# A transformer block with attention and a mixture of experts: a new prelude that builds the first stack on the chip and leaves the rest to the loop

## What is computed

```python
xn = layernorm(x)                                # x is (8, 512, 128): 8 batches of 512 tokens
q, k, v = xn @ Wq.T, xn @ Wk.T, xn @ Wv.T         # 16 heads of 8
q, k = rope(q), rope(k)                          # the angle depends on the batch alone
att = softmax(q @ k.T / sqrt(8)) @ v             # per batch and head
s = sigmoid(xn @ gate_w.T)                       # 32 experts in 8 groups
combine = top 6 experts of the best 4 groups of s + e_bias, weights s / sum * 2.5
moe = sum_e combine_e * relu(xn @ up_e.T)**2 @ down_e.T
shared = relu(xn @ shared_up.T)**2 @ shared_down.T
out = x + att + moe + shared
```

## Time and profile before

| | us |
|---|---|
| median of 3 runs | 686.49 (686.17 to 690.81) |
| the profiled execution | 682.6 |
| its span, first to last instruction | 680.8 |
| TensorE busy in it | 664.0 |
| DVE, ACT, POOL busy | 426.9, 414.4, 421.5 |

### The profile page before, as it was taken

How to read it: one execution, slowest core, us unless ns; L and a number is a source line. 1 busy time by engine, 2 the same in 40 slices (tenths; PEclk the granted TensorE clock), 3 DMA queues, 4 the chain that set the end, 5 groups by cost and what they waited for, 6 DMA issues and landing times. The chain is left out here.

```text
span 680.8 us, 12599 instructions
## 1 busy us (share of the span) xinstructions
PE 664.0 (98%) x4450; PEld 311.2 (46%) x4450; DVE 426.9 (63%) x1055; ACT 414.4 (61%) x771; POOL 421.5 (62%) x461
## 2 busy tenths in 40 slices
PE   7988999999999999999999999999999999999996
PEld 6532444445444444444444444445444444454443
DVE  5783567566865777566765777667756686655300
ACT  2534356665666666666666666766666566666662
POOL 1570347765787567665776668666676576656654
PEclk9997599999999999999999999999999999999999
DMA  7826034543246335633446314734555314332320
GB/s 197 272 78 187 23 72 94 192 124 95 59 110 215 77 76 125 222 95 94 113 108 195 83 44 120 222 94 94 125 159 157 94 43 110 88 79 62 94 64 16
DMA packets 52974, 77.80 MB, mean 114 GB/s; under 512 B 6064, under 2 KB 19248, under 8 KB 52784
## 3 DMA queue, kind: packets, MB, share of 16 engines
q1 hardware_dynamic: 52336, 75.95, 41.7%
q10 hardware_dynamic: 576, 1.05, 0.5%
HBM read 57.19 MB, written 19.40 MB: 112 GB/s over the span
## 5 line engine op out<-in xcount | busy, mean ns | idle before, releaser
L648 DVE TENSOR_REDUCE nmax<-sc 128x1 f32<-128x512 f32 x512 | 330.4, 686 | 195.3 <-PE sc L806 190.7
L472 ACT ACTIVATE probs<-st 128x512 f32<-128x512 f32 x512 | 278.0, 595 | 49.7 <-PE st L822 48.4
L364 POOL TENSOR_TENSOR gated<-gate_at,relu 128x512 f32<-128x512 f32 x128 | 163.3, 1276 | 206.7 <-ACT relu L477 206.7
L368 POOL TENSOR_TENSOR g<-gated,relu 128x512 f32<-128x512 f32 x128 | 163.0, 1274 | 18.5 <-POOL gated L364 0.4
L477 ACT ACTIVATE relu<-upb 128x512 f32<-128x512 f32 x128 | 76.5, 597 | 139.5 <-PE upb L877 139.5
L822 PE MATMUL st<-stacks 32*128 32x512 f32 x512 | 152.8, 575 | 0.0
L847 PE MATMUL acc<-dn,g 128*128 128x128 f32 x1024 | 149.2, 289 | 1.4 <-POOL g L368 1.4
L847 PEld LDWEIGHTS acc<-dn,g 128*128 128x128 f32 x1024 | 124.7, 192 | 45.6 <-issue 44.0
L806 PE MATMUL sc<-stacks 32*128 32x512 f32 x512 | 140.2, 501 | 1.0 <-DVE nmax L648 1.0
L841 PE MATMUL pv<-probs,v_aug 128*32 128x512 f32 x1024 | 138.1, 612 | 0.0
L877 PE MATMUL upb<-xnT,up 128*128 128x512 f32 x256 | 134.0, 606 | 0.0
(11 more groups left out here) (102 smaller groups left out, 399.0 us busy)
## 6 DMA issues: line engine op xcount, KB each, us to landing
gate_at<-gate_rows SPq DMA_DIRECT2D x64, 512.0 KB, 6.5
q_stack<-qk_parts SPq DMA_DIRECT2D x32, 256.0 KB, 6.4
stacks<-q_stack SPq DMA_DIRECT2D x32, 256.0 KB, 4.6
stacks<-k_stack SPq DMA_DIRECT2D x32, 256.0 KB, 5.1
k_stack<-qk_parts SPq DMA_DIRECT2D x28, 256.0 KB, 5.6
gate_at<-in_x SPq DMA_DIRECT2D x8, 256.0 KB, 5.2
x_res<-in_x SPq DMA_DIRECT2D x8, 256.0 KB, 7.0
out<-y SPq DMA_DIRECT2D x8, 256.0 KB, 6.9
```

Of the source, the lines that this page charges most:

```text
L364: nc.gpsimd.tensor_tensor(gated[:, u % 2, :], gate_at[:, group % RING, u % GATES, :], relu[:, u % RELUS, :], ALU.mult).then_inc(gated_read ...
L368: nc.gpsimd.tensor_tensor(g[:, u % 2, :], gated[:, u % 2, :], relu[:, u % RELUS, :], ALU.mult).then_inc(g_ready, 1)
L472: nc.scalar.activation(probs[:, u % 2, h, :], st_b[h % 2][:], ACT.Exp).then_inc(probs_ready, 1)
L648: nc.vector.tensor_reduce(out=nmax[:, s % 2, at:at + 1], in_=sc_b[tile % SC_BANKS][:], op=ALU.max, axis=AXX, negate=True).then_inc(s_read, 1)
```

## The change

The first stack (batch 0, heads 0 to 3) is no longer sent through DRAM. POOL copies the weight columns of its heads four times (`replicate`), PE projects batch 0 with these into rows that already stand in the stack's order (`project_rows`), and DVE writes high or low part of each row by two passes (`first_stack`). The other three stacks of batch 0 still go through DRAM.

Only batches 0 and 1 are transposed and projected in the prelude. Batches 2 to 7 follow in the loop, two batches ahead: transposes in unit 0, q in 4, k in 8, logits in 15; the shared products stand in 7 and 11, v in 3, gates in 12. x of batches 3 to 7 is loaded in the loop; its statistics are taken in units 10 and 11 on DVE, and the inverse root and normalisation in 11 to 14 on POOL, with an exponent of -0.5 (`inverse_std`). The router's gates of batch 0 are computed from piece 4 on in units 0 to 2 and turned in unit 3. The down products start in unit 6 and catch up by two in every second unit (`place_downs`); `RELUS` is 8. Four scores of step 1 are ahead of the loop and not eight, and the first four units take six each.

The sigmoid is now an exponential, an addition of one (`logits_out`), and a reciprocal on DVE in piece 0 of the route. Three operations of the route use a form that also writes an accumulator (`apart`).

```diff
-RELUS = 4
+RELUS = 8
...
-LAG = 2
+LAG, FIRST_LAG = 2, 6
...
-FIRST_AHEAD = 8
+FIRST_AHEAD = 4
+
+FIRST_X = 3
...
+def place_downs():
+
+    done = 0
+    for u in range(FIRST_LAG, UNITS):
+        due = u - LAG + 1
+        n = 2 if u >= FIRST_LAG + 2 and u % 2 == 0 else 1
+        while done < due and n:
+            DOWN_AT[u].append(done)
+            done += 1
+            n -= 1
+
...
+        SHDOWN_UNIT = (4, 6)
+        SQUARE_UNIT, SPLIT_UNIT = (7, 15), (5, 6, 9, 10)
...
+        X_UNIT, V_UNIT, Q_UNIT, K_UNIT, SH_UNIT, GATE_UNIT, LOGIT_UNIT = 0, 3, 4, 8, (7, 11), 12, 15
+
+        V1_UNIT, GATE0_UNIT = 1, 3
...
+        STATS_UNIT, AGGR_UNIT, LN_UNIT, NORM_UNIT = 10, 11, 11, (12, 13, 14, 14)
+
+        ROUTE_MID, ROUTE_END = {3: 2, 4: 3, 7: 5, 8: 6}, {0: 0, 2: 1, 6: 4, 8: 7, 10: 8}
+        ROUTE1_MID, ROUTE1_END = {6: 2, 7: 3, 8: 5, 10: 6}, {4: 0, 5: 1, 7: 4, 10: 7, 11: 8}
+
+        ROUTE0_FIRST, ROUTE0_MID, ROUTE0_END = 4, {1: 5, 2: 7}, {0: 4, 1: 6, 2: 8}
+        ROUTE_AT = (0, 3, 6, 8, 9, 12, 14, 15, 19, 21)
         ROUTE_PIECES, ROUTE_STEPS = len(ROUTE_AT) - 1, ROUTE_AT[-1]
 
 
...
+        WARM_FIRST, WARM_COPY, WARM_CHAIN = 30, 6, 10
+
+        BESIDE = (("v", 0), ("shared", 0), ("shared", 1), ("x", 1), ("q", 1), ("k", 1), ("logits", 1))
+        NW1, NW2, NUP, NALL = 4, 3, 5, 7
...
+            store_rows(0, 0, slice(QUAD, 2 * QUAD), stored_1)
+            store_rows(0, 1, slice(QUAD, 2 * QUAD), stored_1)
+            store_rows(0, 0, slice(2 * QUAD, H), stored_2)
             load_stack(0, 1)
-            sp.dma_start(up[:], upT).then_inc(w2_ld, 16)
+            store_rows(0, 1, slice(2 * QUAD, H), stored_2)
+            load_max(0)
+            load_stack(0, 2)
+            load_stack(0, 3)
             sp.dma_start(sdn[:], shared_down.rearrange("(n p) d -> p n d", p=P)).then_inc(w2_ld, 16)
             sp.dma_start(dn[:], down.rearrange("(n p) d -> p n d", p=P)).then_inc(w2_ld, 16)
-            load_stack(0, 2)
-            load_stack(0, 3)
+            store_parts(1)
+            load_x(FIRST_X)
...
+                    if s == 0:
+                        store_gates(0)
+                        load_gates(0)
...
+            def replicate(w):
+
+                nc.gpsimd.tensor_copy(w_rows[:, w, :].rearrange("p (h c d) -> p h c d", c=COPIES, d=HD),
+                                      (wq, wk)[w][:, 0:QUAD * HD].rearrange("p (h d) -> p h d", d=HD).unsqueeze(2)
+                                      .to_broadcast([P, QUAD, COPIES, HD])).then_inc(rows_ready, 1)
+
+            def inverse_std(batches, first):
+
+                at = slice(batches[0] * TT, (batches[-1] + 1) * TT)
+                n = at.stop - at.start
+                v, inv, p0, t0 = (ln[:, k, at] for k in range(4))
+                step = [first]
+
+                def then(ins):
+                    step[0] += 1
+                    ins.then_inc(ln_step, 1)
+                    pool.wait_ge(ln_step, step[0])
+
+                pool.wait_ge(var_ready, batches[-1] + 1)
+                then(nc.gpsimd.tensor_scalar(v, mv[:, at, 1], 1.0, EPS_LN, ALU.mult, ALU.add))
+                then(nc.gpsimd.tensor_tensor(p0, v, half[:, 0:n], ALU.pow))
+                then(nc.gpsimd.tensor_tensor(t0, p0, p0, ALU.mult))
+                then(nc.gpsimd.tensor_tensor(inv, t0, v, ALU.mult))
+                then(nc.gpsimd.tensor_scalar(t0, inv, -0.5, 1.5, ALU.mult, ALU.add))
+                then(nc.gpsimd.tensor_tensor(inv, p0, t0, ALU.mult))
+
+            def normalise(i, tiles):
+                if i < FIRST_X:
...
+            pool.wait_ge(xn_first, 1)
+            set_v(0)
+            pool.wait_ge(half_ready, 1)
+            inverse_std((1, 2), 0)
+            for k in range(4):
+                split(0, k)
+            normalise(1, range(TT))
+            for i in range(NSH):
+                square(0, i)
+            normalise(2, range(TT))
+            set_v(1)
             for k in range(4):
                 split(1, k)
...
+                if b + FIRST_X < B:
+                    if n == LN_UNIT:
+                        inverse_std((b + FIRST_X,), (b + 1) * LN_STEPS)
+                    tiles = [k for k in range(TT) if NORM_UNIT[k] == n]
+                    if tiles:
+                        normalise(b + FIRST_X, tiles)
...
+            def logits_out(i):
+
+                act.wait_ge(logit_psum, i + 1)
+                tiles = sig[:, i * TT:(i + 1) * TT, :].rearrange("p t e -> p (t e)")
+                nc.scalar.activation(tiles, up_b[:, 0:TT * NE], ACT.Exp, scale=-1.0).then_inc(exp_ready, 1)
+                act.wait_ge(exp_ready, i + 1)
+                nc.scalar.activation(tiles, tiles, ACT.Copy, bias=1.0).then_inc(sig_ready, 1)
...
+            def first_stack(w):
+
+                dve.wait_ge(rows_psum, w + 1)
+                dve.wait_ge(low_ready, 1)
+                src, rows = (pv_b, acc_b)[w], stacks[:, 0, w, :]
+                nc.vector.tensor_scalar(rows, src[:], low_fac[:, w:w + 1], None, ALU.mult).then_inc(stack_low, 1)
+                dve.wait_ge(stack_low, w + 1)
+                nc.vector.scalar_tensor_tensor(rows, src[:], fac[:, w:w + 1], rows.bitcast(F32), ALU.mult, ALU.subtract
+                                               ).then_inc(stack_set, 1)
+
+            def apart(out_at, src, scalar, op):
+
+                return nc.vector.tensor_scalar(out_at, src, scalar, 0.0, op, ALU.max, accum_out=junk[:])
...
+                    then(nc.vector.reciprocal(sig[:, tiles, :], sig[:, tiles, :]))
...
-                    then(nc.vector.tensor_scalar_add(msk[:, :, 0:NE], tmp[:], 0.0))
+                    then(apart(msk[:, :, 0:NE], tmp[:], 0.0, ALU.add))
...
+            for i in (1, 2):
+                stats_of(i)
+                moments(i).then_inc(var_ready, 1)
...
+            cut_max(dve, nc.vector, 0)
...
+            def project_rows(w):
+
+                pe.wait_ge(rows_ready, w + 1)
+                nc.tensor.matmul((pv_b, acc_b)[w][:], w_rows[:, w, :], xnT[:, 0:T], start=True, stop=True
+                                 ).then_inc(rows_psum, 1)
...
+            warm(WARM_FIRST, sc_b[0])
+            transpose_x(0)
+            warm(WARM_COPY, sc_b[0])
+            pe.wait_ge(w_ld, NW1 * 16)
+            pe.wait_ge(xnT_ready, 1)
+            project_rows(0)
+            project_rows(1)
+            project(0, 0)
+            project(0, 1)
+            logits(0)
+            for i in range(TILES // 2):
+                score(2 * i)
+                score(2 * i + 1)
+                for kind, k in BESIDE[i:i + 1]:
+                    beside(kind, k)
+            pe.wait_ge(exp_ready, 2)
             max_transpose(0)
+            pe.wait_ge(qk32_ready, 4)
+            warm(WARM_CHAIN, acc_b)
             for i in range(FIRST_AHEAD):
                 score(TILES + i)
-                for kind, n in BEHIND[i * len(BEHIND) // FIRST_AHEAD:(i + 1) * len(BEHIND) // FIRST_AHEAD]:
-                    prelude(kind, n)
-            pe.wait_ge(qk32_ready, 2 * (B - 1))
...
+            warm(WARM_CHAIN, acc_b)
+            pe.wait_ge(m_ready, 1)
...
+                if u == V1_UNIT:
+                    make_v(1)
+                if u == GATE0_UNIT:
+                    gate_transpose(0)
...
+                if b + 2 < B:
+                    if n == X_UNIT:
+                        transpose_x(b + 2)
+                    if n == Q_UNIT:
+                        project(b + 2, 0)
+                    if n == K_UNIT:
+                        project(b + 2, 1)
+                    if n == LOGIT_UNIT:
+                        logits(b + 2)
+                couple(u, 1)
+                if u == 0:
+                    pe.wait_ge(w2_ld, NUP * 16)
+                if u == FIRST_LAG:
+                    pe.wait_ge(w2_ld, NALL * 16)
+                for e in DOWN_AT[u]:
+                    expert_down(e)
+                if u == FIRST_LAG:
+                    for i in range(NSH):
+                        shared_down(0, i)
+                if b and n in SHDOWN_UNIT:
                     shared_down(b, SHDOWN_UNIT.index(n))
```

More of the change, by code:

```diff
@@ L46 @@
 MAXES = MAX_PARTS
-LAG = 2
+LAG, FIRST_LAG = 2, 6
 SC_BANKS = 3
 AHEAD = 12
-FIRST_AHEAD = 8
+FIRST_AHEAD = 4
+FIRST_X = 3
+LN_STEPS = 6
 SC_HEAD = (2, 3, 0, 1)
 SC_AT = {}
+DOWN_AT = {u: [] for u in range(UNITS)}
 def place_scores():
@@ L64, in place_scores @@
         if u < TT:
-            left = min(left, QUAD + 1)
-        for h in range(QUAD):
-            n = -(-left // (QUAD - h))
-            SC_AT[u, h] = list(range(at, at + n))
+            left = min(left, QUAD + 2)
+        for couple in range(2):
+            n = -(-left // (2 - couple))
+            SC_AT[u, couple] = list(range(at, at + n))
             at += n
@@ L543, in then, with stats_of, moments, invert_first @@
                 dve.wait_ge(link, done[0])
[L545 to L559 removed]
+            def stats_of(i):
+                dve.wait_ge(x_ld[i], 16)
+                at = i * TT if i < FIRST_X else 0
```

(62 more changed lines are left out.)

457 lines of the change are left out of this document (194 added, 263 removed).

## The result

| | before | after |
|---|---|---|
| median of 20 runs, us | 687.26 (686.08 to 690.81) | 692.01 (687.28 to 696.46) |
| the profiled execution | 682.6 | 687.3 |
| its span | 680.8 | 685.2 |
| granted clock over the span, profiled run | 0.977 | 0.975 |

A forecast was written before the change was run, and what follows sets the result against it. TensorE's own work was taken to bound mid-loop, half clock and the first stack's DRAM trip the start. 67.0 + 579.8 + 17.9 = 664.7, clock +8 gives span 672.7, offset to the median: forecast 676.5, range 666 to 690.

The forecast's parts named there:

- the wait behind step 0: After step 0's sixteen scores, PE waits 2.7 us for the transpose of the maxima, longer than the 1.89 before.
- the clock's fall there: PE's clock halves at the wait near 29.8, returns in unit 1, may fall again in units 2 and 3: +8 us.
- The insertions: Work for batches 3 to 7 put into loop units, 0.24 of each hidden: 2.6 us a batch, 12.9 in all.
- the sum: Full-clock time of the changed kernel: 67.0 to unit 5's product, 579.8 behind it, 17.9 added: 664.7 us.
- the 579.8 us of before: Old span from unit 5's product at 101.0 to the end at 680.8, tail included, reused for the changed kernel.
- just enough: GpSimd catching up to lag 2 by unit 14: 13 products of 2.6 and 9 us other work in 45 us.
- The second term: the reciprocal: Reciprocal over 128 columns on DVE in route piece 0: 0.25 in each of seven batches, +1.7, bounds 0 and 4.5.
- The accumulating form: In route piece 4, keeps DVE off the port shared with GpSimd, removing a 0.65 stall in six batches: -3.9 us.
- rival 4: GpSimd's power between gating 11 and 12 in five batches costs 5.8 us or more each: 693.5 us; chance 0.10.
- half of an offset: The median shown lay 3.9 us above the profiled run; +2 was carried into the forecast.
- Rival 1: PE stays at half speed from the start until the down products in unit 6: 683.5 to 689.5 us; chance 0.28.
- Rival 3: In the loop, insertions are not hidden and DVE still stalls: 9.7 us above forecast, 686; chance 0.10.

The follow-up runs named there:

- experiment 3: Changed kernel without the reciprocal over 128 columns in the first route piece (routing differs); one profiled run, 680.15 us.
- Experiment 2: Changed kernel with the cuts of the maxima of steps 2 and 3 on GpSimd, not DVE; 682.66 us, ratio to before 0.9942.
- experiment 11: Changed kernel with GpSimd's products of experts 1 and 6 held back until DVE has written cuts 2 and 3; one profiled run, 690.94 us.
- experiment 4: Changed kernel with the three route operations in plain form again, without accumulator; one profiled run, 693.98 us.
- experiment 5: Changed kernel with the power on GpSimd done four times, not once, in each inverse root; one profiled run, 715.4 us.
- experiment 1: Changed kernel with 22 warm-up transposes filling TensorE's wait behind step 0's scores; 690.29 us, ratio to before 1.0048.
- experiments 2 and 9: The latter: changed kernel, cuts on GpSimd, early exponential table, 22 warm-ups in the gap, eight in each of units 0 to 3, route pieces respread; 675.63 us, ratio 0.9825.

## Why the prediction was wrong

**Right.** The first projection (10.7; 11.20) and first score (15.3; 15.62), the wait for the exponential (0.9; 1.22), the wait behind step 0 (2.7; 2.30), the clock's fall there and its price: unit 5's product at 75, measured 74.2. Up to there 27 us are gained, 26 were reckoned. The insertions: x 0.35 (0.36 forecast), q and k 0.82 each (0.82). One power hidden. The stall of 0.65 in unit 5 is gone, and `msk` near 0.25 (0.29). In part the 74.2 is luck. Unit 3's product came at 64.46, where the sum has 59.3 and 8 for the clock, and units 4 and 5 then took 9.7 us for the 7.7 of the sum, 0.86 of it by the reciprocal that stands before unit 5 (experiment 3). Nor was DVE without idle in units 0 to 3: from 57.3 to 64.1 it was busy for 4.72 of 6.80. (Two slips of the sum, 59.8 carried on as 59.3 and a product at 72.3 called 5.5 and not 5.3 later, change nothing.)

**The step that failed first: the stretch behind unit 5's product.** I took the 579.8 us of before and added work to it, as if batch 0 from unit 6 on were in the state it had at 101.00. It is not. Before, GpSimd's first products waited for the relus, one pair a unit (line 364 at 70.62, 77.28 and 87.57), and the cuts of these steps were GpSimd's own, in order with them. The change gives those of batch 0 to DVE. The gates, forecast for 67.6, came 5.6 us later, and the products start at 73.2, one behind the other, just as DVE has to cut the maxima of step 2. I wrote that GpSimd was "just enough" and never asked what DVE does beside it. The cut stood in the sum as 1.55 to 1.7; it takes 3.3. With the row maxima behind it, that makes two waits of 1.78 and 1.70 and 3.4 us at the half clock, which cost 1.7: 5.5 us in unit 6 (the three terms give 5.2), and 2.0 in unit 10, behind a wait of 1.88. Experiment 2 gets 5.8 of these back (7.56 and 5.54), experiment 11 shows the cause, and experiment 3 shows unit 6 without the meeting (8.01). The Trainium skill says it outright, SBUF — State Buffer, Who interferes with whom: a DVE instruction with two inputs in SBUF contends with a GpSimd instruction that reads SBUF, and casts can do so too. These traces agree: 1.20 and 1.12 us beside a product, 0.17 without one. I used that section for one operation of the route, where it changed nothing, and not for the operations that share the time with the products that the change moves.

**The second term: the reciprocal.** Sized well (0.95; 0.94), placed wrongly: I took 0.25 a batch, with 0 to 4.5 in all as bounds. It stands ahead of two row maxima in unit 1, where there was no slack, and costs 4.9 in all (experiment 3), just above the upper bound, and 0.86 more in unit 5 of batch 0. **The logits:** 0.78 and not 0.57, 0.2 in each of five batches. **The accumulating form:** the 3.9 came, but not from the form (experiment 4). **Unit 14:** the wait of 0.78 for GpSimd behind the power in batch 0, 0.9 in the end, is rival 4's mechanism in the one batch in which GpSimd was still catching up; in the other batches my margin was a little too large: 2.4 for the power less its 1.03 is 1.4, and experiment 5 leaves some 1 us.

**The clock.** In the profiled run it was as I took it: back in unit 1, and down once more in units 2 and 3. That is in part luck too, as experiment 1 tells. But before's median of 20 lies 4.7 above its profiled run (687.26 and 682.6), and after's as well; I carried half of an offset that is there as a whole. The spread has grown too: the 20 runs of after have a granted clock of 0.953 to 0.975, with the profiled one at the upper end. Four runs at 0.958 took 694.7 to 695.2, two at 0.975 687.3. A difference of 0.017 over 690 us is 2 x 0.017 x 690 = 23 us more at half speed, for 7.7 us more time. The traces of experiments 1 and 3 show falls at 81.6, 103.1 and 108.9 besides those of the start, and that of experiment 3 one at 17.8. Which of these the 695 us runs had cannot be read, as only one execution has a trace.

**The rivals.** None was it. Rival 1 (half speed until the products come, 683.5 to 689.5) came nearest in time, not in mechanism: the clock was back twice before unit 6, and the 13 us were lost behind it. Rival 3 had the right sign for DVE in the loop and the wrong place. What the list lacked is the wait that takes the place of the one removed, in the middle: gates and products that had waited for PE now came when PE was already there, all at once, next to another engine's chain.

## What to carry to other kernels

Moving work earlier on one engine moves it onto other neighbours: list, for each stretch that shifts, what every engine does beside it, before the old trace's time for that stretch is used again. Small DVE operations in a chain that PE waits for belong in a place where GpSimd is idle, or on GpSimd itself. And where the clock's falls differ from one execution to the next, one trace does not tell what a filled gap is worth: compare medians and the granted clocks of many executions. Here filling one gap brought next to nothing (experiment 1); with the early table and the warm-ups in the units the medians fell from 682.66 to 675.63 (experiments 2 and 9), some 2 us of which are the route pieces' new places.
